# The last feed-forward of a two-layer decoder: the output product made transposed, in rounded halves, inside the sequence of wide products

## The chip, the cores and the metric

One core of one Trainium2 chip runs the whole program in one launch. Its engines work beside each other and meet only at semaphores: TensorE (PE in the rows; its weight loads stand apart as PEld), VectorE (DVE), ScalarE (ACT), GpSimd (POOL) and SyncE (SP), which starts the transfers. The metric is the device time of one execution in microseconds. It is compared as the median of several runs.

## What is computed

Two decoder layers in fp32 on `x` of 16 x 112 x 256. The change lies in the last step of the last layer, a feed-forward whose two largest of four gates choose a low-rank correction:

```python
logits = jnp.einsum('bsd,ed->bse', x, Wg) + bg
scores = jax.nn.softmax(logits, axis=-1)
topv, topi = jax.lax.top_k(scores, TOP_K)            # TOP_K = 2 of E = 4
w = jnp.sum(jax.nn.one_hot(topi, E) * topv[..., None], axis=-2)
base = jnp.einsum('bsd,fd->bsf', x, Wi)              # 256 -> 1024
lora = jnp.einsum('bser,efr->bsef', jnp.einsum('bsd,erd->bser', x, A), B)   # rank 4
h = jax.nn.relu(base[:, :, None, :] + lora)
expert_out = jnp.einsum('bsef,df->bsed', h, Wo)      # 1024 -> 256
out = jnp.einsum('bse,bsed->bsd', w, expert_out)
```

The `x` here is the normalised stream, and `out` is added to the stream itself. The output product is linear, so the kernel weighs the two chosen `h` of a token first and multiplies by `Wo` once.

## The kernel before

The function `l1_experts` is the last phase. It handles the 16 batch elements in four groups `g` of four, so a group has 4 x 112 = 448 tokens (`GT`). The 1024 inner features are cut into eight blocks `f` of 128 (`FC`), so the phase has 32 steps. Within one step of the loop over `f`:

- TensorE makes `z` (128 features x 448 tokens) in fp32 from two halves of the input (`multiply_wide`, L2774) and adds the first choice's low-rank term in one product of the rounded type fp32r (`multiply_low`, L2780). A second such product, `change` (L2786), holds the difference between the two choices.
- ScalarE copies `z` out of PSUM (`take_first`, L2724).
- VectorE adds `change` (L2663), applies relu and the weight ratio (L2666), and adds the first choice's relu (L2671). The result is block `f` of `h`. All eight blocks of a group are kept.

TensorE issues the wide and low product two blocks ahead. After the eight steps comes `project_out` (L2819): for each of the four batch elements eight fp32 products with the tokens' `h` as the weights and 256 columns of `Wo` moving, so that the output has tokens on the partitions. It is 32 products for a group, in one piece. VectorE weighs each result and adds the stream (`take_result`, L2679), and SyncE stores a group when its four results stand. Between the groups lie small things: `transpose_one_hot` (L2759) and `spread_ratio` (L2766) on TensorE, `mask_low` (L2623), `split_low` (L2629), `find_best` (L2642 to L2653) and `take_shares` (L2612 to L2615) on VectorE, `round_low` (L2713) and `take_ratio` (L2718) on ScalarE.

"Rounded halves" are a way to make an accurate product from the faster type: a number is written as a rounded part `hi` (a ScalarE copy into fp32r) and the rest `lo` (a subtraction), and three products hi x hi, lo x hi and hi x lo replace one fp32 product. The kernel does so already in the cross-attention of the first layer (L1037 to L1039, 488 columns, and L1046 to L1048, 512 columns).

Each engine runs its own list in the order written, and an instruction that waits holds up everything behind it on its engine. PSUM has eight banks of 512 columns: two for `z`, two for `change`, two for `y`, one each for the two one-hot tiles.

Of the kernel before, what the change touches and what calls it, by code (L numbers as in the profile page):

```python
# [7 lines left out]
F32 = mybir.dt.float32  # L8
# [2529 lines left out]
def l1_experts(nc, x, stats, norms, w, gate, ident, passed, A, out):  # L2538
# [16 lines left out]
    FIRST_SHARES, LAST_SHARES = slice(0, B - 2 * GB), slice(B - 2 * GB, B)  # L2555
# [4 lines left out]
    with ExitStack() as ctx:  # L2560
# [6 lines left out]
        h = ph.sb("h", [128, FC, GT])  # L2567
# [3 lines left out]
        z_ps, change_ps, y_ps = ph.banks("z", 2), ph.banks("change", 2), ph.banks("y", 2)  # L2571
# [12 lines left out]
        h_step, y_done, x_step = ph.sem("h_step"), ph.sem("y_done"), ph.sem("x_step")  # L2584

# [22 lines left out]
        @block.vector  # L2608
        def _(dve):
# [47 lines left out]
            def activate(g, f):  # L2657
                n = g * FC + f
# [4 lines left out]
                nc.vector.tensor_tensor(z_second[:, f % 2, :], z_first[:, f % 4, :], change_ps[:, f % 2, 0:GT], ALU.add  # L2663
                                        ).then_inc(h_step, 1)
# [4 lines left out]
                if f == 0:  # L2669
                    since(dve, y_done, g * GB)  # L2670
                nc.vector.scalar_tensor_tensor(h[:, f, :], z_first[:, f % 4, :], 0.0, z_second[:, f % 2, :], ALU.max, ALU.add  # L2671
                                               ).then_inc(h_step, 1)

            def take_result(g, j):
                b = g * GB + j
                dve.wait_ge(y_done, b + 1)
                if j == 0:
                    since(dve, stored[g % 2], g // 2 * 16)
                nc.vector.scalar_tensor_tensor(result[:, g % 2, j, :], y_ps[0:S, j % 2, 0:D], weight[:, b:b + 1], x[:, b, :],  # L2679
                                               ALU.mult, ALU.add).then_inc(x_step, 1)  # L2680
# [4 lines left out]
            take_shares(0, FIRST_SHARES)  # L2685
# [4 lines left out]
            for g in range(G):  # L2690
                for f in range(FC):
                    activate(g, f)
                    if g == 0 and f == 1:
                        take_gate()
                if g + 1 < G:
                    mask_low(g + 1)
                    split_low(g + 1)
                take_result(g, 0)
                if g == 0:
                    find_best(0, G - 2)  # L2700
                    find_best(1, G - 1)
                elif g == 1:
                    take_shares(1, LAST_SHARES)
                for j in range(1, GB):
                    take_result(g, j)

        @block.scalar
        def _(act):
# [17 lines left out]
            nc.scalar.activation(share[:, FIRST_SHARES], share[:, FIRST_SHARES], ACT.Exp).then_inc(exp_ready, 1)  # L2726
# [9 lines left out]
            for g in range(G):  # L2736
                for f in range(FC):
                    take_first(g, f)
                    if g == 0 and f == 2:
                        act.wait_ge(gate_done, 1)  # L2740
                        nc.scalar.activation(low[:, (G - 1) * GT:G * GT], y_ps[0:ER, 0, 0:GT], ACT.Copy).then_inc(low_ready, 1)
                if g + 1 < G:
                    round_low(g + 1)
                    if g == 1:
                        act.wait_ge(share_ready, 2)
                        nc.scalar.activation(share[:, LAST_SHARES], share[:, LAST_SHARES], ACT.Exp).then_inc(exp_ready, 1)
                    take_ratio(g + 1)

        @block.tensor
        def _(pe):  # L2750
# [11 lines left out]
            def spread_ratio(g):  # L2762
                pe.wait_ge(ratio_ready, 2 if g >= 2 else 1)
# [19 lines left out]
            def multiply_change(g, f):  # L2783
                n = g * FC + f
                since(pe, h_step, n * 3 - 5)
                nc.tensor.matmul(change_ps[:, f % 2, 0:GT], low_b_r[:, f * 128:(f + 1) * 128], low_change[:, g % 2],  # L2786
                                 start=True, stop=True).then_inc(change_done, 1)
# [9 lines left out]
            def multiply_gate():  # L2797
# [7 lines left out]
                for c in range(KC):  # L2805
                    done = nc.tensor.matmul(y_ps[0:ER, 0, 0:GT], low_a[:, c, :], x1T[:, c, (G - 1) * GT:G * GT],  # L2806
                                            start=(c == 0), stop=(c == KC - 1))
                done.then_inc(gate_done, 1)

            def project_out(g):  # L2810
                if g == 0:
                    pe.wait_ge(low_ready, 1)
                for j in range(GB):
                    b = g * GB + j
                    since(pe, x_step, b - 1)
                    for f in range(FC):
# [11 lines left out]
            for g in range(G):  # L2828
                multiply_low(g, 0)
                multiply_low(g, 1)  # L2830
                for f in range(FC):
                    multiply_change(g, f)
                    if f + 2 < FC:
                        multiply_wide(g, f + 2)
                        multiply_low(g, f + 2)
                    if g == 0 and f == 0:
                        multiply_gate()
                if g + 1 < G:
                    transpose_one_hot(g + 1)
                    multiply_wide(g + 1, 0)  # L2840
                    multiply_wide(g + 1, 1)
                project_out(g)
                if g + 1 < G:
                    spread_ratio(g + 1)

# [109 lines left out]
```

## Time and profile before

| | |
|---|---|
| Median of 3 runs | 1724.64 us (1720.76 to 1724.70) |
| Profiled execution, its own time | 1724.28 us |
| Its span in the trace | 1722.4 us |
| TensorE busy over the span | 1632.5 us (95%) |
| VectorE, ScalarE, GpSimd busy | 1084.2, 776.1, 544.8 us |
| Mean granted TensorE clock | 0.983 |
| Last feed-forward, first product to end of span | 1584.9 to 1722.4 us |

Rows of the timeline give the start of an instruction or of a run of equal ones, and its length. A TensorE record reaches from issue to the end of its pipeline, so records overlap: the price of a product in a dense stretch is the distance between starts, not the length. An fp32 product has two matmul records; an fp32r product has one. Span and own time differ by 1.88 us that lie outside the trace.

### The profile page before, as it was taken

How to read it: one execution, taken by the hardware profiler on the slowest of the kernel's cores; microseconds unless marked ns; L12 is line 12 of the kernel's file. 1: busy time of each engine (PE TensorE's matmuls, PEld its weight loads, DVE VectorE, ACT ScalarE, POOL GpSimd, SP SyncE). 2: the span in 40 equal slices, each digit the busy share in tenths (PEclk: the TensorE clock that was granted, in tenths of full speed). 3: DMA queues.
4: the chain of work that ended last, by engine and by line, in shares of the span. 5: the costliest groups of instructions: out<-in, count | busy, mean ns of one | idle time of the engine just before them, and what ended most of it. 6: DMA issues, size and time to landing. Idle time of an engine off the chain costs nothing. (4 is left out here: it accounts for less than half of the span.)

```text
span 1722.4 us, 33298 instructions
## 1 busy us (share of the span) xinstructions
PE 1632.5 (95%) x11494; PEld 1313.1 (76%) x11494; DVE 1084.2 (63%) x2543; ACT 776.1 (45%) x2178; POOL 544.8 (32%) x581
## 2 busy tenths in 40 slices
PE   6999899999999999999999988899988899988998
PEld 6877678778778878777887866799977777655666
DVE  5566467666777666667676664455354578856664
ACT  2356354444454455454545441365402577743211
POOL 1022223333333333333333334244430033354000
PEclk9999999999999999999999999899998999998999
DMA  3100300000000000000001004575310000010000
GB/s 102 48 11 1 117 12 11 11 10 10 0 10 10 10 10 10 8 2 10 10 10 55 11 2 167 140 255 191 104 64 21 25 2 2 2 60 1 11 11 22
DMA packets 48808, 67.46 MB, mean 39 GB/s; under 512 B 11826, under 2 KB 42770, under 8 KB 46034
## 3 DMA queue, kind: packets, MB, share of 16 engines
q1 hardware_dynamic: 47186, 62.66, 11.6%
q0 software_dynamic: 1536, 3.67, 0.7%
q8 instruction: 51, 0.84, 0.2%
q14 instruction: 35, 0.29, 0.1%
HBM read 57.02 MB, written 9.31 MB: 39 GB/s over the span
## 5 line engine op out<-in xcount | busy, mean ns | idle before, releaser
L709 POOL TENSOR_TENSOR l0x_p<-l0x_p,l0x_inv 112x488 f32<-112x488 f32 x256 | 261.7, 1043 | 426.4 <-DVE l0x_inv L806 425.2
L934 ACT ACTIVATE l0x_p<-l0x_s,l0x_low 112x488 f32<-112x488 f32 x256 | 177.9, 696 | 255.3 <-DVE l0x_low L795 222.6
L795 DVE CUSTOM_DVE_ANT_0 l0x_s<-l0x_score_ps,l0x_bias 112x488 f32<-112x488 f32 x256 | 160.2, 664 | 95.0 <-PE l0x_score_ps L1081 85.7
L1102 PE MATMUL l0x_oT_ps<-l0x_pT,l0x_v 122*64 122x112 f32 x2048 | 127.2, 266 | 7.0 <-ACT l0x_pT L940 6.1
L1089 PEld LDWEIGHTS l0x_pT_ps<-ident,l0x_p 112*122 112x122 f32 x1024 | 99.0, 138 | 45.3 <-issue 39.2
L1102 PEld LDWEIGHTS l0x_oT_ps<-l0x_pT,l0x_v 122*64 122x64 f32 x2048 | 99.6, 137 | 42.5 <-issue 31.8
L1089 PE MATMUL l0x_pT_ps<-ident,l0x_p 112*122 112x112 f32 x1024 | 126.1, 266 | 0.4 <-POOL l0x_p L709 0.3
L782 DVE TENSOR_TENSOR l0x_kT_lo<-l0x_proj_ps,l0x_kT_hi 128x488 fp32r<-128x488 f32 x128 | 84.1, 667 | 63.2 <-ACT l0x_kT_hi L924 63.2
L1037 PE MATMUL l0x_proj_ps<-l0x_kvT_hi,l0x_wkv_hi 128*128 128x488 f32 x256 | 104.7, 409 | 2.9 <-DVE l0x_kvT_lo L770 2.9
L1046 PE MATMUL l0x_proj_ps<-l0x_wkv_hi,l0x_kvT_hi 128*122 128x512 f32 x256 | 105.2, 411 | 0.0
L1047 PE MATMUL l0x_proj_ps<-l0x_wkv_lo,l0x_kvT_hi 128*122 128x512 f32 x256 | 101.0, 395 | 0.0
L1048 PE MATMUL l0x_proj_ps<-l0x_wkv_hi,l0x_kvT_lo 128*122 128x512 f32 x256 | 100.9, 394 | 0.0
L1039 PE MATMUL l0x_proj_ps<-l0x_kvT_hi,l0x_wkv_lo 128*128 128x488 f32 x256 | 99.4, 388 | 0.0
L1038 PE MATMUL l0x_proj_ps<-l0x_kvT_lo,l0x_wkv_hi 128*128 128x488 f32 x256 | 99.3, 388 | 0.0
L924 ACT ACTIVATE l0x_kT_hi<-l0x_proj_ps 128x488 fp32r<-128x488 f32 x128 | 72.9, 571 | 27.5 <-PE l0x_proj_ps L1039 27.4
L801 DVE COPY l0x_pT<-l0x_pT_ps 122x448 f32<-122x448 f32 x128 | 79.2, 619 | 4.6 <-PE l0x_pT_ps L1089 4.6
L1731 PE MATMUL l0f_hT_ps<-l0f_xsT,l0f_w 128*128 128x128 f32 x672 | 80.2, 279 | 0.0
L1731 PEld LDWEIGHTS l0f_hT_ps<-l0f_xsT,l0f_w 128*128 128x128 f32 x672 | 78.3, 195 | 0.0
L2040 POOL TENSOR_TENSOR l1a_pn<-l1a_p_even,l1a_inv 112x896 f32<-112x896 f32 x16 | 26.9, 1683 | 137.8 <-POOLq L1887 99.0
L211 ACT ACTIVATE l0a_p<-l0a_p,l0a_shift 112x112 f32<-112x112 f32 x128 | 47.8, 374 | 45.9 <-DVE l0a_shift L201 45.6
L940 ACT ACTIVATE l0x_pT<-l0x_pT_ps 122x448 f32<-122x448 f32 x128 | 66.7, 521 | 1.8 <-PE l0x_pT_ps L1089 1.8
L218 POOL TENSOR_TENSOR l0a_pn<-l0a_p,l0a_inv 112x896 f32<-112x896 f32 x16 | 26.9, 1683 | 120.3 <-DVE l0a_inv L206 120.3
(392 smaller groups left out, 4045.6 us busy)
## 6 DMA issues: line engine op xcount, KB each, us to landing
l0f_w<-in_l0f_w SPq DMA_DIRECT2D x21, 1024.0 KB
l0x_c_in<-in_ctx SPq DMA_DIRECT2D x16, 375.0 KB
l1x_gram_context<-in_ctx SPq DMA_DIRECT2D x16, 375.0 KB
sorted_x<-l0x_zeros SPq DMA_DIRECT2D x1, 2816.0 KB, 15.3
l0f_xs<-sorted_x SPq DMA_DIRECT2D x21, 128.0 KB, 2.2
sorted_y<-l0f_z SPq DMA_DIRECT2D x21, 128.0 KB, 1.8
l0x_wkv<-in_l0x_wkv SPq DMA_DIRECT2D x2, 1024.0 KB, 9.2
x<-in_x SPq DMA_DIRECT2D x4, 448.0 KB, 7.8
```

The source lines that it names most:

```text
L709: nc.gpsimd.tensor_tensor(p[:, i % 2, a, :], p[:, i % 2, a, :], inv[:, i % 2, a:a + 1].broadcast_to([S, KEYS]), ALU.mult).then_inc(pn_read ...
L795: nc.vector.tensor_tensor_reduce(s_sb[:, h % 2, :], score_ps[0:S, h % 2, 0:KEYS], bias[:], -SCALE, 3.4e38, ALU.add, ALU.min, low[:, h:h + ...
L934: nc.scalar.activation(p[:, h // 2 % 2, h % 2, :], s_sb[:, h % 2, :], ACT.Exp, scale=-1.0, bias=low[:, h:h + 1], accum_out=total[:, h:h + ...
L1037: nc.tensor.matmul(out, wkv_hi[:, c, at], kvT_hi[:, c, :], start=(c == 0), stop=False)
L1038: nc.tensor.matmul(out, wkv_hi[:, c, at], kvT_lo[:, c, :], start=False, stop=False)
L1039: done = nc.tensor.matmul(out, wkv_lo[:, c, at], kvT_hi[:, c, :], start=False, stop=(c == KC - 1))
L1046: nc.tensor.matmul(out, kvT_hi[:, c, keys], wkv_hi[:, c, at], start=(c == 0), stop=False)
L1047: nc.tensor.matmul(out, kvT_hi[:, c, keys], wkv_lo[:, c, at], start=False, stop=False)
L1048: done = nc.tensor.matmul(out, kvT_lo[:, c, keys], wkv_hi[:, c, at], start=False, stop=(c == KC - 1))
L1089: done = nc.tensor.transpose(pT_ps[0:KT, a, t * S:(t + 1) * S], p[:, i % 2, a, t * KT:(t + 1) * KT], ident[0:S, 0:S])
L1102: done = nc.tensor.matmul(oT_ps[a * DH:(a + 1) * DH, 0, (i % 4) * S:(i % 4 + 1) * S], v[:, t, (2 * i + a) * DH:(2 * i + a + 1) * DH], pT[: ...
L1731: done = nc.tensor.matmul(hT_ps[:, 2 * (i % 2) + f // 4, (f % 4) * 128:(f % 4 + 1) * 128], w1[:, i % 3, c, f * 128:(f + 1) * 128], xsT[:, ...
```

## The change

`project_out` is no longer a piece for a group. It becomes one of six products for each of the 32 steps, issued two steps after the step that made its `h`. `Wo` blocks are now the weights and `h` (448 columns) moves, so the output `yT` has features on the partitions. Operands are fp32r halves: `h_hi` comes from ScalarE (`round_h`), `h_lo` from VectorE (`split_h`). `Wo` is halved once at the start, by ScalarE and GpSimd. When a group's last block has been added, ScalarE copies `yT` out of PSUM (`take_yT`), TensorE turns it back (`transpose_back`: two transposes for a batch element, eight for a group, in two parts) and VectorE takes the results during steps 2 and 3 of the next group. `h` shrinks from eight blocks to two, `change` from two banks to one (its freed bank holds `back`). `find_best`, `take_shares`, `mask_low` and `split_low` are spread over steps 2 to 5. The shares are taken in three pieces instead of two.

```diff
+            for f in range(FC):
+                pool.wait_ge(wo_hi_ready, f + 1)
+                nc.gpsimd.tensor_tensor(wo_lo[:, f, :], wo[:, f, :], wo_hi[:, f, :].bitcast(F32), ALU.subtract
+                                        ).then_inc(wo_lo_ready, 1)
...
+            def split_h(n):
+                dve.wait_ge(h_hi_ready, n + 1)
+                nc.vector.tensor_tensor(h_lo[:, n % 3, :], h[:, n % 2, :], h_hi[:, n % 3, :].bitcast(F32), ALU.subtract
+                                        ).then_inc(h_lo_ready, 1)
...
-            for g in range(G):
-                for f in range(FC):
-                    activate(g, f)
-                    if g == 0 and f == 1:
-                        take_gate()
-                if g + 1 < G:
+            for n in range(STEPS):
+                g, f = divmod(n, FC)
+                activate(n)
+                if n >= 1:
+                    split_h(n - 1)
+                if n == 1:
+                    take_gate()
+                if g >= 1 and f in (2, 3):
+                    take_result(g - 1, 2 * f - 4)
+                    take_result(g - 1, 2 * f - 3)
+                if f == 2 and 1 <= g <= 2:
+                    take_shares(g, SHARES[g])
+                if f == 3 and g + 1 < G:
                     mask_low(g + 1)
+                if f == 4 and g + 1 < G:
                     split_low(g + 1)
-                take_result(g, 0)
...
+                if f == 5 and g < 2:
+                    find_best(g, G - 2 + g)
+            split_h(STEPS - 1)
+            for j in range(GB):
+                take_result(G - 1, j)
...
+            take_first(0, 0)
+            take_first(0, 1)
+            for f in range(FC):
+                nc.scalar.activation(wo_hi[:, f, :], wo[:, f, :], ACT.Copy).then_inc(wo_hi_ready, 1)
+            for n in range(STEPS):
+                g, f = divmod(n, FC)
+                if n + 2 < STEPS:
+                    take_first(*divmod(n + 2, FC))
...
+                if g >= 1 and f == 1:
+                    take_yT(g - 1)
+                round_h(n)
...
             def multiply_change(g, f):
                 n = g * FC + f
-                since(pe, h_step, n * 3 - 5)
...
+                since(pe, h_step, n * 3 - 2)
...
-            def project_out(g):
-                if g == 0:
+            def project_out(n):
+                g, f = divmod(n, FC)
+                if n == 0:
+                    pe.wait_ge(wo_lo_ready, FC)
+                pe.wait_ge(h_lo_ready, n + 1)
...
+                hi, lo = h_hi[:, n % 3, :], h_lo[:, n % 3, :]
+                for c in range(KC):
+                    if f == 0:
+                        since(pe, yT_ready, (g - 1) * KC + c + 1)
+                    at = slice(c * 128, (c + 1) * 128)
+                    nc.tensor.matmul(y_ps[:, c, 0:GT], wo_hi[:, f, at], hi, start=(f == 0), stop=False)
+                    nc.tensor.matmul(y_ps[:, c, 0:GT], wo_lo[:, f, at], hi, start=False, stop=False)
+                    done = nc.tensor.matmul(y_ps[:, c, 0:GT], wo_hi[:, f, at], lo, start=False, stop=(f == FC - 1))
...
+            def transpose_back(g, part):
...
+                pe.wait_ge(yT_ready, (g + 1) * KC)
+                since(pe, x_step, g * GB + 2 * part)
+                for j in (2 * part, 2 * part + 1):
+                    for c in range(KC):
+                        at = (j % 2) * D + c * 128
+                        done = nc.tensor.transpose(back_ps[0:S, 0, at:at + 128], yT[:, c, j * S:(j + 1) * S], ident[:])
                     done.then_inc(y_done, 1)
...
+            for n in range(STEPS):
+                g, f = divmod(n, FC)
+                multiply_change(g, f)
+                if n + 2 < STEPS:
+                    multiply_wide(*divmod(n + 2, FC))
+                    multiply_low(*divmod(n + 2, FC))
...
+                if g >= 1 and f in (2, 3):
+                    transpose_back(g - 1, f - 2)
+                if n >= 2:
+                    project_out(n - 2)
```

TensorE at the end of group 0 in the kernel before: `l1f_z_ps` is the wide and low product, `l1f_y_ps` the output product, the rows with `ident` the small transposes.

```order
 L2774 MATMUL l1f_z_ps<-l1f_x1T,l1f_wi 128x448 x2
 L2780 MATMUL l1f_z_ps<-l1f_low_first,l1f_low_b_r 128x448
 L2786 MATMUL l1f_change_ps<-l1f_low_change,l1f_low_b_r 128x448 x2
 L2759 MATMUL l1f_first_hot_ps<-ident,l1f_one_hot 80x112 x4
 L2759 MATMUL l1f_change_hot_ps<-ident,l1f_one_hot 80x112 x4
 L2774 MATMUL l1f_z_ps<-l1f_x1T,l1f_wi 128x448 x4
 L2819 MATMUL l1f_y_ps<-l1f_wo,l1f_h 112x256 x32
 L2766 MATMUL l1f_change_hot_ps<-ident,l1f_ratio 128x112 x4
 L2780 MATMUL l1f_z_ps<-l1f_low_first,l1f_low_b_r 128x448 x2
```

TensorE in the changed kernel, step 2 of group 1, where the turning back stands (`l1f_back_ps`):

```order
 L2835 MATMUL l1f_change_ps<-l1f_low_change,l1f_low_b_r 128x448
 L2823 MATMUL l1f_z_ps<-l1f_x1T,l1f_wi 128x448 x2
 L2829 MATMUL l1f_z_ps<-l1f_low_first,l1f_low_b_r 128x448
 L2887 MATMUL l1f_back_ps<-ident,l1f_yT 112x128 x4
 L2871 MATMUL l1f_y_ps<-l1f_h_hi,l1f_wo_hi 128x448
 L2872 MATMUL l1f_y_ps<-l1f_h_hi,l1f_wo_lo 128x448
 L2873 MATMUL l1f_y_ps<-l1f_h_lo,l1f_wo_hi 128x448
 L2871 MATMUL l1f_y_ps<-l1f_h_hi,l1f_wo_hi 128x448
 L2872 MATMUL l1f_y_ps<-l1f_h_hi,l1f_wo_lo 128x448
 L2873 MATMUL l1f_y_ps<-l1f_h_lo,l1f_wo_hi 128x448
```

The 32 products in one row have become six in each step, and the wide product no longer runs ahead of a long piece.

VectorE in the changed kernel, steps 2 and 3 of the last group (`l1f_h_lo` is `split_h`, `l1f_result` is `take_result`; the kernel before has the three lines of a step alone and `l1f_result` x4 after the last step):

```order
 L2678 SCALAR_TENSOR_TENSOR l1f_z_second<-l1f_z_second,l1f_ratio_rows 128x448
 L2681 SCALAR_TENSOR_TENSOR l1f_h<-l1f_z_first,l1f_z_second 128x448
 L2686 TENSOR_TENSOR l1f_h_lo<-l1f_h,l1f_h_hi 128x448
 L2694 SCALAR_TENSOR_TENSOR l1f_result<-l1f_back_ps,l1f_weight,x 112x256 x2
 L2675 TENSOR_TENSOR l1f_z_second<-l1f_z_first,l1f_change_ps 128x448
 L2678 SCALAR_TENSOR_TENSOR l1f_z_second<-l1f_z_second,l1f_ratio_rows 128x448
```

A step has four long operations on VectorE instead of three, and results stand between the steps.

ScalarE in the changed kernel, from the first step of group 2 (`l1f_h_hi` is `round_h`, `l1f_yT` is `take_yT`):

```order
 L2744 ACTIVATE l1f_z_first<-l1f_z_ps 128x448
 L2764 ACTIVATE l1f_yT<-l1f_y_ps 128x448 x2
 L2758 ACTIVATE l1f_h_hi<-l1f_h 128x448
 L2744 ACTIVATE l1f_z_first<-l1f_z_ps 128x448
 L2758 ACTIVATE l1f_h_hi<-l1f_h 128x448
```

The copy of `yT` stands ahead of step 1's rounding, which waits behind it.

## Rows read from the trace of the kernel before

**Rows 1.** The page: engines over the span; busy us, share, instructions.
```profile
PE 1632.5 (95%) x11494; PEld 1313.1 (76%) x11494; DVE 1084.2 (63%) x2543; ACT 776.1 (45%) x2178; POOL 544.8 (32%) x581
```
**Rows 2.** Windows of the last phase: length, busy PE, PEld, DVE, ACT, POOL, clock, DMA.
```profile
1584.00:1600.00 16.00, 14.30 (x66) 9.70 (x66) 5.97 (x17) 7.10 (x14) 1.82 (x3) 0.86 0.01 1
...
1612.20:1626.10 13.90, 13.90 (x66) 11.37 (x65) 7.41 (x38) 1.11 (x2) 1.72 (x2) 1.00 0.01 2
```
**Rows 3.** Timeline, group 0: start, length, engine, line, out<-in.
```profile
1595.65 0.54 ACT L2724 ACTIVATE l1f_z_first<-l1f_z_ps 128x448 f32<-128x448 f32 x1 [1.62 <-PE l1f_z_ps L2780]
1600.41 0.36 PE L2786 MATMUL l1f_change_ps<-l1f_low_change,l1f_low_b_r 80*128 80x448 f32 x1
...
1602.33 0.36 PE L2786 MATMUL l1f_change_ps<-l1f_low_change,l1f_low_b_r 80*128 80x448 f32 x1
...
1602.53 1.67 PE L2774 MATMUL l1f_z_ps<-l1f_x1T,l1f_wi 128*128 128x448 f32 x4
1602.79 0.62 DVE L2663 TENSOR_TENSOR l1f_z_second<-l1f_z_first,l1f_change_ps 128x448 f32<-128x448 f32 x1
1603.45 0.62 DVE L2666 SCALAR_TENSOR_TENSOR l1f_z_second<-l1f_z_second,l1f_ratio_rows 128x448 f32<-128x448 f32 x1
...
1608.05 0.57 PE L2786 MATMUL l1f_change_ps<-l1f_low_change,l1f_low_b_r 80*128 80x448 f32 x2
...
1608.46 0.55 PE L2759 MATMUL l1f_first_hot_ps<-ident,l1f_one_hot 112*80 112x112 f32 x4
```
**Rows 4.** Timeline, between groups 0 and 1, TensorE alone.
```profile
1609.23 3.19 PE L2774 MATMUL l1f_z_ps<-l1f_x1T,l1f_wi 128*128 128x448 f32 x8
1612.25 13.98 PE L2819 MATMUL l1f_y_ps<-l1f_wo,l1f_h 128*112 128x256 f32 x64
1626.07 1.04 PE L2766 MATMUL l1f_change_hot_ps<-ident,l1f_ratio 112*128 112x112 f32 x8
1626.88 0.65 PE L2780 MATMUL l1f_z_ps<-l1f_low_first,l1f_low_b_r 80*128 80x448 f32 x2
1627.37 0.37 PE L2786 MATMUL l1f_change_ps<-l1f_low_change,l1f_low_b_r 80*128 80x448 f32 x1
1628.18 1.77 PE L2774 MATMUL l1f_z_ps<-l1f_x1T,l1f_wi 128*128 128x448 f32 x4 [0.44 <-ACT l1f_z_first L2724]
```
**Rows 5.** Timeline, rounded products of the first layer's cross-attention, 488 columns.
```profile
602.01 0.38 PE L1038 MATMUL l0x_proj_ps<-l0x_kvT_lo,l0x_wkv_hi 128*128 128x488 f32 x1
...
604.22 0.39 PE L1039 MATMUL l0x_proj_ps<-l0x_kvT_hi,l0x_wkv_lo 128*128 128x488 f32 x1
```
**Rows 6.** Timeline, VectorE and ScalarE at the end of group 0.
```profile
1611.69 0.62 DVE L2671 SCALAR_TENSOR_TENSOR l1f_h<-l1f_z_first,l1f_z_second 128x448 f32<-128x448 f32 x1
1612.23 0.61 DVE L2623 TENSOR_TENSOR l1f_low_masked<-l1f_low,l1f_first_hot_ps 80x448 f32<-80x448 f32 x1
...
1612.88 0.58 ACT L2713 ACTIVATE l1f_low_first<-l1f_low_masked 80x448 fp32r<-80x448 f32 x1 [4.08 <-DVE l1f_low_masked L2623]
1613.41 0.58 ACT L2713 ACTIVATE l1f_low_change<-l1f_low_masked 80x448 fp32r<-80x448 f32 x1
1613.49 0.62 DVE L2629 TENSOR_TENSOR l1f_low_first<-l1f_low_masked,l1f_low_first 16x448 fp32r<-16x448 f32 x1
```
**Rows 7.** Timeline, GpSimd and VectorE in the phase before, two groups of it.
```profile
1546.76 3.20 POOL L2271 TENSOR_TENSOR l1x_y_in<-l0f_x,l1x_rows 112x256 f32<-112x256 f32 x4
...
1548.01 2.63 DVE L2354 SCALAR_TENSOR_TENSOR l1x_z<-l1x_y,l1x_y_mv,l1x_rows 112x256 f32<-112x256 f32 x4
...
1558.98 2.79 POOL L2271 TENSOR_TENSOR l1x_y_in<-l0f_x,l1x_rows 112x256 f32<-112x256 f32 x4
...
1563.65 1.67 DVE L2354 SCALAR_TENSOR_TENSOR l1x_z<-l1x_y,l1x_y_mv,l1x_rows 112x256 f32<-112x256 f32 x4
```
**Rows 8.** Timeline, the end of the span.
```profile
1707.17 11.04 PE L2819 MATMUL l1f_y_ps<-l1f_wo,l1f_h 128*112 128x256 f32 x50 [1.08 <-DVE l1f_h L2671]
...
1718.25 0.48 DVE L2679 SCALAR_TENSOR_TENSOR l1f_result<-l1f_y_ps,l1f_weight,x 112x256 f32<-112x256 f32 x1 [2.97 <-PE l1f_y_ps L2819]
```

More of the change, by code:

```diff
@@ L2566, in l1_experts @@
         z_first, z_second = ph.sb("z_first", [128, 4, GT]), ph.sb("z_second", [128, 2, GT])
-        h = ph.sb("h", [128, FC, GT])
+        h = ph.sb("h", [128, 2, GT])
+        h_hi, h_lo = ph.sb("h_hi", [128, 3, GT], F32R), ph.sb("h_lo", [128, 3, GT], F32R)
+        wo_hi, wo_lo = ph.sb("wo_hi", [128, FC, D], F32R), ph.sb("wo_lo", [128, FC, D], F32R)
+        yT = ph.sb("yT", [128, KC, GT])
         result = ph.sb("result", [S, 2, GB, D])
-        z_ps, change_ps, y_ps = ph.banks("z", 2), ph.banks("change", 2), ph.banks("y", 2)
+        z_ps, change_ps, y_ps = ph.banks("z", 2), ph.banks("change", 1), ph.banks("y", 2)
+        back_ps = ph.banks("back", 1)
         first_hot_ps, change_hot_ps = ph.banks("first_hot", 1), ph.banks("change_hot", 1)
@@ L2735, in _ @@
             nc.scalar.activation(x1T[:, :, (G - 1) * GT:G * GT], y_ps[:, :, 0:GT], ACT.Copy).then_inc(xT_ready, 1)
[L2736 to L2742, printed above, removed]
+            take_first(0, 0)
[7 more added lines that the diff above has]
+                if n == 0:
+                    act.wait_ge(gate_done, 1)
+                    nc.scalar.activation(low[:, (G - 1) * GT:G * GT], back_ps[0:ER, 0, 0:GT], ACT.Copy).then_inc(low_ready, 1)
+                if g >= 1 and f == 1:
+                    take_yT(g - 1)
+                round_h(n)
+                if f == 0 and 1 <= g <= 2:
+                    weigh_shares(g)
+                if f == 3 and g + 1 < G:
                     round_low(g + 1)
-                    if g == 1:
-                        act.wait_ge(share_ready, 2)
-                        nc.scalar.activation(share[:, LAST_SHARES], share[:, LAST_SHARES], ACT.Exp).then_inc(exp_ready, 1)
+                if f == 5 and g + 1 < G:
                     take_ratio(g + 1)
+            take_yT(G - 1)
         @block.tensor
@@ new lines, in transpose_back @@
+            def transpose_back(g, part):
+                if g == 0 and part == 0:
+                    pe.wait_ge(low_ready, 1)
+                pe.wait_ge(yT_ready, (g + 1) * KC)
+                since(pe, x_step, g * GB + 2 * part)
+                for j in (2 * part, 2 * part + 1):
+                    for c in range(KC):
+                        at = (j % 2) * D + c * 128
+                        done = nc.tensor.transpose(back_ps[0:S, 0, at:at + 128], yT[:, c, j * S:(j + 1) * S], ident[:])
@@ L2827, in _ @@
             transpose_last()
[L2828 to L2838, printed above, removed]
+            multiply_low(0, 0)
+            multiply_low(0, 1)
+            for n in range(STEPS):
+                g, f = divmod(n, FC)
+                multiply_change(g, f)
+                if n + 2 < STEPS:
+                    multiply_wide(*divmod(n + 2, FC))
+                    multiply_low(*divmod(n + 2, FC))
+                if n == 0:
+                    multiply_gate()
+                if g >= 1 and f in (2, 3):
+                    transpose_back(g - 1, f - 2)
+                if n >= 2:
+                    project_out(n - 2)
+                if f == 2 and g + 1 < G:
                     transpose_one_hot(g + 1)
[L2840 to L2843, printed above, removed]
+                if f == 5 and g + 1 < G:
                     spread_ratio(g + 1)
+            project_out(STEPS - 2)
+            project_out(STEPS - 1)
+            transpose_back(G - 1, 0)
+            transpose_back(G - 1, 1)
 def program(nc, A, out):
```

67 lines of the change are left out of this document (38 added, 29 removed).

## The prediction

> **What bounds the kernel now.** I read the page's first part: TensorE is busy 95% of the span [rows 1]. That alone says little, so I laid out the last phase in the timeline. Inside a group, `change` starts at 1600.41 and again at 1602.33 with TensorE never idle; over the steps that follow the distance is 1.905 us, since from the start at 1600.41 to the one at 1608.05 there are four steps, 7.64 us [rows 3]. So a step costs TensorE 1.905 us, VectorE and ScalarE wait for it. One rounded product of 448 columns costs 0.205 us: two stand between 1608.05 and 1608.46 [rows 3]. The wide product is the rest, 1.905 - 2 x 0.205 = 1.495 us for two fp32 products. After the eight steps, the 32 output products run from 1612.25 to 1626.07, 13.82 us, or 0.432 each, with no gap [rows 4]. Behind them TensorE is briefly starved: `change` starts at 1627.37 and the next wide product only at 1628.18, 0.6 us more than its own price [rows 4]. The clock is at 2.4 GHz in that stretch (granted 1.00); at the phase's beginning it is 0.86 of it on average [rows 2]. TensorE's work is therefore what sets the end, down to the last result at 1718.25 [rows 8].
>
> **Removed.** 128 fp32 products x 0.432 = 55.3 us of TensorE, all on the path. Three joints between groups of 0.6 to 0.7 us each, since the next group's wide product is now issued while the old group's output is still being made: 2 us. Before the last group's output TensorE waits for `h` as well: 1707.17 is such a start [rows 8]; about 1.5 us.
>
> **Added on TensorE.** 32 steps x 6 rounded products. Price from 0.205 us (same width, 80 rows) [rows 3]. The nearest rows with 128 rows and this very pattern of halves have 488 columns: ten intervals from 602.01 to 604.22, 0.221 us each [rows 5]. Scaled by the columns that is 0.203; unscaled 0.221 is the upper end. I take 0.205: 192 x 0.205 = 39.4 us, upper end 42.4, lower end 38. A step is then 1.905 + 1.23 = 3.135 us. The turning back is 32 transposes; eight similar ones (112 wide instead of 128) take 1608.46 to 1609.23, 0.77 us [rows 3, 4], so 0.77 for a group.
>
> **The start.** Up to step 1 nothing on TensorE changes, and both kernels should meet at the `change` of step 2, 1600.41 [rows 3]. What is new must be ready by its output products at 1600.41 + 1.905 = 1602.3. ScalarE now rounds eight blocks of `Wo` (256 columns) before its third `take_first`, which stood at 1595.65 [rows 3]. An activation from SBUF of 448 columns follows its like after 0.53 us [rows 6], so eight take 3 to 4 us from 1594.1 and end by 1598.4; the third `take_first` slips to 1598.9, and its reader, the wide product two steps on, comes at 1600.6. Hidden, with 1.7 us to spare. GpSimd subtracts eight blocks: a 112 x 256 one costs 2.79 / 4 = 0.70 us [rows 7], 5.6 us from 1594.5, end 1600.1. But in the phase before, where GpSimd and VectorE each read two SBUF tensors at once, four GpSimd operations took 3.20 instead of 2.79 us and four of VectorE 2.63 instead of 1.67 [rows 7]. VectorE runs five such operations here. So the end can move to 1601 to 1603.4, and `h_lo` of step 0, due at about 1601.5, can slip by 1 us. I take 0.5 us of waiting on TensorE, bounds 0 and 1.5.
>
> The Trainium skill ("SBUF — State Buffer", section "SBUF: two separate sides") says more: one of the two engines holds the shared port pair for its whole instruction and the other blocks. If the trace followed that fully, 5.6 us and five operations of 0.62 us would stand in line to 1603.2, and the wait would be 0.9 us instead of 0.5. Rows 7 show a part of this, the sign agrees.
>
> **The middle.** From 1600.41: steps 2 to 29 are 28 x 3.135 = 87.8 us. To it come, three times each, the one-hot transposes (0.77), the spreading of the ratio (1626.07 to 1626.88, 0.81 [rows 4]) and the turning back (0.77): 7.05 us. With the 0.5 us, step 30 starts at 1695.7.
>
> Does VectorE keep up? An operation that waits for the one before starts 0.66 us after it (1602.79 and 1603.45, [rows 3]), one that does not, 0.54 us after (1611.69 and 1612.23, [rows 6]). A step is then add, multiply, maximum and `split_h`: 0.66 + 0.66 + 0.54 + 0.54 = 2.40 us against 3.135. Rounding the rest of `h` is like L2629, 0.62 us long at the same width [rows 6]. The small operations of a group are at most the 7.41 us that stand beside the first output piece [rows 2]. So 8 x 2.40 + 7.4 = 26.6 against 8 x 3.135 + 2.35 = 27.4 us on TensorE: it keeps up, by little. The small ones land in steps 2 to 5, where VectorE has 4 x 0.735 = 2.9 us to spare and TensorE's own extras give 2.35: 2.1 us late at the worst. It may be some 2 us late: the single `change` bank lets TensorE go on when the add is done (0.46 + 0.62 us into a step of 3.135), and `h_lo` of step n is ready 3 us into step n + 1 and wanted 1.9 us into step n + 2, 2.0 us later. In groups 0 and 1 the two meet: 0 to 0.2 us each, which I leave out; if VectorE's operations were a tenth longer it would be about 1.5 us each, and that is the upper end, 3 us.
>
> A rule of the Trainium skill ("VectorE: DVE Perf Modes", section "The DRAIN you can't avoid") has a semaphore between two operations cost nothing. The rows say 0.12 us each. By the rule a VectorE step would be 2.16 us, and the tail below 0.6 us shorter.
>
> ScalarE has two 0.53 us operations a step. Its long wait is at step 1 of a group: `take_yT` waits for TensorE's end of the step, and `round_h` of step 1 waits behind it. It is done 1.7 us into step 2; VectorE wants it some 2.5 us into step 2. Hidden; its cover is gone if TensorE is ahead of VectorE by nothing. `transpose_back` in step 2 waits for both copies, ready 1.2 us in, and stands 1.7 us in behind the wide product: also hidden.
>
> **The tail.** After 1695.7 there is no wide product to hide behind. Counted from there, by the intervals above: the step's add 0.46, its `h` done 2.40, `h_lo` of step 29 done 2.93 (TensorE, at 1.64, waits 1.3), step 31's `h` done 4.79, `h_lo` of step 30 done 5.32 (TensorE waits 1.2 more), of step 31 6.06. The last six products run 6.58 to 7.98, the copies of `yT` end at 8.56, the first four transposes at 9.12, two results at 10.1, and only then may the second four go, since `back` has one bank: results end at 11.6. TensorE does 6.1 us of work in these 11.6. So the last result ends at 1707.3, where it was 1718.73 [rows 8]; from there to the end of the span lie 3.67 us of storing in both. Span 1711.0, own time 1711.0 + 1.88 = 1712.9 against 1724.28 of the profiled execution; the median lies 0.4 above that one, so **1713**. A second way to count it: 55.3 + 2 + 1.5 - 39.4 - 3.1 = 16.3 us, less 0.5 at the start and 5 of idle at the end, is 10.8 us, beside 11.4 the first way. This difference is my rounding.
>
> **Rivals.**
> - *VectorE becomes the bound.* For it: 26.6 against 27.4 us leaves 3%, and the clustering in steps 2 to 5. Against it: TensorE has room for a lag of 2 us. Each VectorE operation 10% longer costs 3 us (1716); 20% longer makes VectorE set the pace in three groups, 8 x 0.48 - 0.8 = 3 us for each, 9 in all with the tail's 1: 1723. I give 0.15 to 1716 to 1719.5 and 0.06 to more.
> - *Slower than before: the rounded products do not overlap with their weight loads.* Each of the 192 has its own load now, where a load served a longer product. If each took its record's whole length, 0.38 us [rows 5], that is 192 x 0.175 = 33.6 us more: 1746. It decides from 0.264 us a product on. Against it: rows 5 have records of 0.38 and starts every 0.22. 0.04.
> - *The sequence does not do what it says*: the shorter products come, but TensorE waits in each step for the chain over VectorE, ScalarE and VectorE to `h_lo`. The chain has a whole step of room by the count above; 0.3 us a step would be 10 us, 1722. 0.03.
> - *More than forecast*: products at 0.195, no wait at the start, less in the tail: 1710. Part of the forecast's own range.
>
> **How the numbers follow.** The forecast, 1710 to 1716, has 0.72. Before's three runs spread over 4 us, which also enters. The range 1709 to 1718.5 takes in the product price (-1.5, +3), the start (+1) and most of the VectorE case. About 0.3% is what a measurement of this kernel can tell from no change, 5.2 us: faster is below 1719.5. Faster 0.72 + 0.15 = 0.87; the third rival and half of the heavy VectorE case are within, 0.08; slower 0.05.
>
> **What would show it.** Right: `change` every 3.1 to 3.15 us in steady steps; six starts of L2871 to L2873 0.205 apart; VectorE busy 75% to 95% in the phase; TensorE idle over 1 us only after the last wide product; the first output product at about 1602.8. Wrong: idle time of TensorE before L2835 (the `change` bank) or L2871 (`h_lo`) in steps 4 to 7 of groups 0 and 1; product starts over 0.22 apart; a tail of more than 12 us from step 30 to the last result.

## The result, and the profile after

| | before | changed |
|---|---|---|
| Median of 8 runs | 1725.32 us (1720.76 to 1728.20) | 1714.65 us (1709.31 to 1722.63) |
| Profiled execution: own time, span | 1724.28, 1722.4 us | 1714.85, 1713.0 us |
| `change` of step 2 to end of the last result | 1600.41 to 1718.73: 118.32 us | 1600.19 to 1709.40: 109.21 us |

The ratio is 0.9948, with a 95% interval of 0.9932 to 0.9965, which lies below 1: faster, by half a per cent. The third line of the table is the measure of most that follows, because the eight runs of each kernel spread over 7 and 13 us and part of that arises before this phase: over the profiled executions, whose code before the phase is the same, its first product starts at 1582.11 to 1588.85. I call that third line **the stage**.

From the page of the changed kernel, its engines (busy us, share of the span, instructions), to be read beside [rows 1]:

```profile
PE 1622.8 (95%) x11462; PEld 1309.2 (76%) x11462; DVE 1100.7 (64%) x2578; ACT 800.7 (47%) x2227; POOL 552.0 (32%) x589
```

TensorE has 9.7 us less, VectorE 16.5 and ScalarE 24.6 us more, and TensorE still is the engine that sets the end. The window over the dense part of the phase (length, then busy time with instructions of PE, PEld, DVE, ACT and POOL, granted clock, DMA share, GB/s):

```profile
1602.30:1694.00 91.70, 91.70 (x396) 67.96 (x394) 81.06 (x170) 37.06 (x71) 1.76 (x2) 1.00 0.05 16
```

TensorE is busy for all of the 91.70 us and VectorE for 88% of them. The timeline of TensorE at the start of the phase and of a step later, the counterpart of [rows 3]:

```profile
1600.19 0.36 PE L2835 MATMUL l1f_change_ps<-l1f_low_change,l1f_low_b_r 80*128 80x448 f32 x1
...
1602.09 0.37 PE L2871 MATMUL l1f_y_ps<-l1f_h_hi,l1f_wo_hi 128*128 128x448 f32 x1
1602.30 0.37 PE L2872 MATMUL l1f_y_ps<-l1f_h_hi,l1f_wo_lo 128*128 128x448 f32 x1
...
1607.23 0.36 PE L2835 MATMUL l1f_change_ps<-l1f_low_change,l1f_low_b_r 80*128 80x448 f32 x1
...
1610.36 0.36 PE L2835 MATMUL l1f_change_ps<-l1f_low_change,l1f_low_b_r 80*128 80x448 f32 x1
...
1695.62 0.36 PE L2835 MATMUL l1f_change_ps<-l1f_low_change,l1f_low_b_r 80*128 80x448 f32 x1
```

The first output product stands 1.90 us after `change`, so it waits for nothing. The six products start 0.20 to 0.21 us apart, a step takes 3.13 us, and step 30 starts at 1695.62. GpSimd and VectorE at the start, while `Wo` is halved; the second line is the view of the tile `l1f_wo_lo` (shortest, median and longest of the eight, in ns):

```profile
1594.17 6.66 POOL L2612 TENSOR_TENSOR l1f_wo_lo<-l1f_wo,l1f_wo_hi 128x256 fp32r<-128x256 f32 x8 [7.69 <-ACT l1f_wo_hi L2779]
...
L2612 POOL TENSOR_TENSOR l1f_wo_lo<-l1f_wo,l1f_wo_hi x8: 724/733/1121, 1594.2 to 1599.7; 128x256 fp32r<-128x256 f32 x8
...
1594.70 1.04 DVE L2681 SCALAR_TENSOR_TENSOR l1f_h<-l1f_z_first,l1f_z_second 128x448 f32<-128x448 f32 x1
...
1600.28 1.04 DVE L2681 SCALAR_TENSOR_TENSOR l1f_h<-l1f_z_first,l1f_z_second 128x448 f32<-128x448 f32 x1
1601.24 0.61 DVE L2686 TENSOR_TENSOR l1f_h_lo<-l1f_h,l1f_h_hi 128x448 fp32r<-128x448 f32 x1
...
1603.16 0.63 DVE L2681 SCALAR_TENSOR_TENSOR l1f_h<-l1f_z_first,l1f_z_second 128x448 f32<-128x448 f32 x1
```

Eight subtractions take 6.66 us. Their mean of 0.83 hides two kinds: five are 0.72 to 0.73 us long and start 0.68 us apart, about as the undisturbed ones in [rows 7], and the three that stand beside VectorE's L2678 and L2681 (at 1594.17, 1595.22 and 1599.71) take 1.09 to 1.12. VectorE's L2681 takes 1.04 us there and 0.63 afterwards. GpSimd ends at 1600.83, 1.3 us before the first reader; `h_lo` of step 0 ends at 1601.85, only 0.24 us before its reader at 1602.09. Now the end of the phase, TensorE's waits first (us in brackets, behind them who released it):

```profile
1698.62 0.47 PE L2871 MATMUL l1f_y_ps<-l1f_h_hi,l1f_wo_hi 128*128 128x448 f32 x1 [1.20 <-DVE l1f_h_lo L2686]
...
1701.01 0.74 PE L2871 MATMUL l1f_y_ps<-l1f_h_hi,l1f_wo_hi 128*128 128x448 f32 x1 [0.88 <-DVE l1f_h_lo L2686]
...
1701.54 0.58 PE L2872 MATMUL l1f_y_ps<-l1f_h_hi,l1f_wo_lo 128*128 128x448 f32 x1
1701.92 0.58 PE L2873 MATMUL l1f_y_ps<-l1f_h_lo,l1f_wo_hi 128*128 128x448 f32 x1
...
1707.49 0.99 PE L2887 MATMUL l1f_back_ps<-ident,l1f_yT 128*112 128x128 f32 x4 [1.06 <-DVE l1f_result L2694]
1708.52 0.88 DVE L2694 SCALAR_TENSOR_TENSOR l1f_result<-l1f_back_ps,l1f_weight,x 112x256 f32<-112x256 f32 x2 [1.17 <-PE l1f_back_ps L2887]
```

And windows of the same kernel over that place (the last two lines are narrower ones):

```profile
1695.00:1701.00 6.00, 3.92 (x18) 2.93 (x16) 5.16 (x9) 1.74 (x4) 0.00 (x0) 0.98 0.00 0
1701.00:1705.00 4.00, 4.00 (x12) 3.42 (x12) 0.62 (x1) 0.44 (x2) 0.00 (x0) 0.60 0.00 0
1701.00:1704.00 3.00, 3.00 (x8) 2.72 (x9) 0.62 (x1) 0.02 (x1) 0.00 (x0) 0.50 0.00 0
1707.50:1708.50 1.00, 0.98 (x4) 0.57 (x4) 0.00 (x0) 0.00 (x0) 0.00 (x0) 0.55 0.00 0
```

The two waits were forecast, the rows behind the second are not: the products start 0.37 to 0.38 us apart instead of 0.205, and the granted clock is 0.50, the level of 1.2 GHz, from 1701 to 1704 (0.60 on average over four us). From 1704.4 on they stand 0.20 apart again. A second, smaller fall, to 0.55, lies over the last four transposes, behind their own wait of 1.06 us. The tail (step 30's `change` to the last result's end) is 13.78 us, where 11.6 was forecast.

### The profile page after: what moved, and what is told of

Its sections match the earlier page's. It is cut to its first block and busy times, and to the rows that moved or that the text cites. A ratio compares the mean times of both kernels' runs of the same rounds, so it can differ in the third digit from the quotient of the medians.

```text
span 1713.0 us, 33366 instructions
## 1 busy us (share of the span) xinstructions
PE 1622.8 (95%) x11462; PEld 1309.2 (76%) x11462; DVE 1100.7 (64%) x2578; ACT 800.7 (47%) x2227; POOL 552.0 (32%) x589
## 3 DMA queue, kind: packets, MB, share of 16 engines
q1 hardware_dynamic: 47186, 62.66, 11.8%
HBM read 57.02 MB, written 9.31 MB: 39 GB/s over the span
```

## The experiments

Each kernel was profiled once, the changed one twice. Its stage, its tail, and its ratio to the kernel before, whose tail includes the last piece of output products:

| kernel | stage, us | tail, us | ratio (95%) |
|---|---|---|---|
| before | 118.32 | 16.23 | 1 |
| changed, first profile | 109.21 | 13.78 | 0.9948 (0.9932 to 0.9965) |
| c0, changed again | 107.39 | 11.97 | 0.9942 (0.9918 to 0.9966) |
| e1, woven, fp32 | 113.81 | 10.81 | 0.9968 (0.9949 to 0.9986) |
| e6, one piece, transposed fp32 | 122.72 | 18.07 | 1.0025 (1.0014 to 1.0037) |
| e4, VectorE +1 operation a step | 113.16 | 13.10 | 0.9969 (0.9946 to 0.9992) |
| e3, tail filled | 107.34 | 11.96 | 0.9937 (0.9920 to 0.9954) |
| e8, longer waits | 111.63 | 16.26 | 0.9958 (0.9918 to 0.9998) |
| e9, longer waits, filled | 109.50 | 14.11 | 0.9964 (0.9943 to 0.9984) |
| e2, last three steps fp32 | 105.64 | 10.21 | 0.9917 (0.9896 to 0.9938) |
| e7, e2 and a shorter end | 104.71 | 9.31 | 0.9911 (0.9884 to 0.9938) |

### c0_changed: the same kernel once more

> The changed kernel itself, on the chip on which the next three run, so that they have a neighbour. Expected 9 to 12 us below the kernel before, span near 1713, the last feed-forward's tail (from the change product of step 30 to the last result) 13.4 us long.

Same ratio. The end of the phase in this second profile, timeline and a window:

```profile
1700.03 0.47 PE L2871 MATMUL l1f_y_ps<-l1f_h_hi,l1f_wo_hi 128*128 128x448 f32 x1 [0.90 <-DVE l1f_h_lo L2686]
...
1700.33 0.37 PE L2872 MATMUL l1f_y_ps<-l1f_h_hi,l1f_wo_lo 128*128 128x448 f32 x1
...
1705.73 0.88 DVE L2694 SCALAR_TENSOR_TENSOR l1f_result<-l1f_back_ps,l1f_weight,x 112x256 f32<-112x256 f32 x2 [0.81 <-PE l1f_back_ps L2887]
```

```profile
1700.00:1704.00 4.00, 3.34 (x16) 2.58 (x16) 0.63 (x1) 1.14 (x3) 0.00 (x0) 1.00 0.00 0
```

The same waits to 0.02 us, but the clock stays at 1.00 and the products at 0.20. The tail is 11.97 us, where I had expected 13.4. So the fall of the clock costs 1.8 us where it comes, and it does not come in every execution. Of the 1.8, about 1.45 lies between the first and the last of the twelve output products behind the second wait (3.78 us against 2.33) and 0.37 at the last four transposes (1.03 us from their start to the next result, against 0.66).

### e1_woven_fp32: the weaving without the rounding

```diff
-                    nc.tensor.matmul(y_ps[:, c, 0:GT], wo_hi[:, f, at], hi, start=(f == 0), stop=False)
-                    nc.tensor.matmul(y_ps[:, c, 0:GT], wo_lo[:, f, at], hi, start=False, stop=False)
-                    done = nc.tensor.matmul(y_ps[:, c, 0:GT], wo_hi[:, f, at], lo, start=False, stop=(f == FC - 1))
+                    done = nc.tensor.matmul(y_ps[:, c, 0:GT], wo[:, f, at], h[:, n % 3, :], start=(f == 0), stop=(f == FC - 1))
```

> The woven sequence and the transposed output are kept, the rounding is undone: the output product of a step is two fp32 products of 448 columns on h itself, nothing is rounded or split. Theory (the gain has three parts: orientation, rounding, weaving): an fp32 product of 448 columns costs 0.748 us, so a step of TensorE grows from 3.135 to 3.40 us, 28 steps by 7.4 us; the tail is shorter by about 3 us since no rounding stands in its chain and the clock does not fall. So about 4 us slower than the changed kernel and about 6 us faster than before. Rival (the rounded halves are the whole gain): as slow as before or slower. Rival (VectorE sets the pace of the changed kernel): faster than the changed kernel, since VectorE has three long operations instead of four.

The last step of the timeline (`change`, the four matmul records of the two output products, `change`):

```profile
1702.05 0.71 PE L2829 MATMUL l1f_change_ps<-l1f_low_change,l1f_low_b_r 80*128 80x448 f32 x1
...
1704.30 1.67 PE L2862 MATMUL l1f_y_ps<-l1f_h,l1f_wo 128*128 128x448 f32 x4
...
1705.46 0.71 PE L2829 MATMUL l1f_change_ps<-l1f_low_change,l1f_low_b_r 80*128 80x448 f32 x1
```

A step is 3.41 us, 0.27 more than with rounded halves; the tail is 1.2 us shorter, since no halves have to be made (and a little more than that, as a `change` behind an fp32 product is recorded early, 0.71 us long instead of 0.36). Against c0 the stage is 6.4 us longer.

### e6_piece_fp32: transposed output, still one piece for a group

```diff
-                if n >= 2:
-                    project_out(n - 2)
+                if g >= 1 and f == 1:
+                    for m in range((g - 1) * FC, g * FC):
+                        project_out(m)
```

Products in fp32 as in e1, ten blocks of `h` instead of three.

> As e1_woven_fp32 (transposed output in two fp32 products of 448 columns a step, nothing rounded), but the sixteen output products of a group are issued in one piece of 12.0 us, in step 1 of the next group, and not woven. VectorE's small operations stay in steps 2 to 5. Theory (weaving itself is worth what it hides of VectorE's and ScalarE's work): TensorE's products are the same, but a step now takes 1.905 us beside VectorE's 1.86 us, so the 2 to 6 us of small operations in steps 2 to 5 are no longer covered: TensorE waits about 2, 3 and 1 us in groups 0, 1 and 2, and the last group's twelve us of output follow its last h: about 6 us slower than e1_woven_fp32. Rival (TensorE's sum is all that counts, the order of it nothing): the same as e1_woven_fp32 within 1 us. Rival (weaving alone is the gain of the change, orientation nothing): as slow as the kernel before or slower.

TensorE's waits of this kernel (total, times, longest), and one of them in its timeline:

```profile
PE l1f_change_ps L2829 <- DVE l1f_z_second L2669: 5.7, 5, 1.6
```

```profile
1645.81 0.47 PE L2829 MATMUL l1f_change_ps<-l1f_low_change,l1f_low_b_r 80*128 80x448 f32 x1 [1.56 <-DVE l1f_z_second L2669]
```

By TensorE's price alone the transposed form is cheaper than before: 64 fp32 products of 448 columns, 0.748 each by the wide product's two in 1.495 us [rows 3], are 47.9 us where 55.3 were. Yet the stage is 4.4 us longer than before, and the ratio says slower as well, so 11.8 us have come on. With the output in one piece, TensorE's steps are 1.91 us again. VectorE's three operations of a step take about 1.86, and nothing is left for the small ones of steps 2 to 5; `find_best` alone stands 1.9 us long in step 5 (1610.10 to 1611.99). The single `change` bank passes that lag on to TensorE: 5.7 us. Turning back between the groups is 3 x 0.77 = 2.3 us by the forecast's price. The tail is 18.07 us where the kernel before has 16.23, although its products are 1.85 us cheaper: 3.7 us of turning back and copying behind the last piece.

From e6 to e1 the stage falls by 8.9 us and from e1 to c0 by 6.4; 4.4 - 8.9 - 6.4 = -10.9, the whole from before to c0. The 6.4 is the rounding, in a woven sequence. The 8.9 is not weaving alone: e6 keeps the small operations in steps 2 to 5, where the kernel before has them beside the long piece, so up to the 5.7 us of waits may belong to their place. A piece with the small operations beside it was not run, nor was rounding without weaving, which would need all eight blocks of `h_hi` and `h_lo` at once. I had expected 6 us between e6 and e1.

### e4_vector_once: one more VectorE operation a step

```diff
                     split_h(n - 1)
+                dve.wait_ge(h_step, n * 3 + 3)
+                for k in range(1):
+                    nc.vector.tensor_tensor(z_second[:, f % 2, :], h[:, n % 2, :], h[:, n % 2, :], ALU.add)
```

> The changed kernel with one more VectorE operation of 448 columns in each of the 32 steps, behind split_h, whose result nobody reads: 0.54 us more a step, 17.3 us in all. Theory (TensorE is the bound and VectorE has 3.135 - 2.40 = 0.73 us a step to spare, of which the small operations of steps 2 to 5 take nearly all): steps without small ones stay at 3.13 us; TensorE waits before change or before the output product in steps 4 to 7, nothing in group 0, about 2 us in group 1, 1 in group 2, 0 to 1 in group 3, and the tail grows by 1.1: 4 to 5 us slower than the changed kernel. Rival (VectorE already sets the pace): 15 to 17 us slower. Rival (VectorE has ample room): below 2 us.

Waits of TensorE in this kernel:

```profile
PE l1f_change_ps L2838 <- DVE l1f_z_second L2675: 2.8, 2, 1.4
PE l1f_y_ps L2874 <- DVE l1f_h_lo L2686: 3.0, 3, 1.4
```

In the tail of this kernel, timeline and a window:

```profile
1701.84 0.47 PE L2874 MATMUL l1f_y_ps<-l1f_h_hi,l1f_wo_hi 128*128 128x448 f32 x1 [1.24 <-DVE l1f_h_lo L2686]
...
1704.76 0.47 PE L2874 MATMUL l1f_y_ps<-l1f_h_hi,l1f_wo_hi 128*128 128x448 f32 x1 [1.43 <-DVE l1f_h_lo L2686]
...
1700.00:1708.00 8.00, 4.79 (x21) 3.44 (x20) 5.67 (x10) 2.20 (x4) 0.00 (x0) 1.00 0.00 0
```

The stage is 5.8 us longer than c0's: two steps of group 0 (4.72 and 3.42 us instead of 3.22 and 3.14) and two of group 1 (4.81 and 3.42 instead of 3.21 and 3.13) bring 3.7, the tail 1.1, the rest is spread; the forecast was 4 to 5. Thirty-two operations of more than 0.5 us are over 16 us, and about two thirds of it still fit beside TensorE. So TensorE is the bound, and VectorE's slack is real but small: 0.5 us a step is more than it holds in two of the four groups. I had expected no loss in group 0. The tail shows one thing more: waits of 1.24 and 1.43 us, longer than those of the changed kernel, and the clock stayed at 1.00.

### e3_tail_filled: the waits of the tail filled with unread products

```diff
+            def fill(count):
+                pe.wait_ge(first_ready, STEPS)
+                for k in range(count):
+                    nc.tensor.matmul(z_ps[:, 0, 0:GT], low_b_r[:, 0:128], low_change[:, (G - 1) % 2], start=True, stop=True)
```

Six stand ahead of step 29's output products and five ahead of step 30's.

> The changed kernel with eleven more rounded products in the tail whose results nobody reads (six before the output products of step 29, five before those of step 30), in the time in which TensorE waited. Theory (the waits bring the clock down): the clock stays at 1.00 in the last output products, which are 0.205 us apart instead of 0.373, and the span is about 1.5 us shorter than that of the changed kernel although TensorE does more. Rival (the clock falls there anyway, or the products are slow for another reason): the same span or up to 2 us more.

Tail 11.96 us, clock 1.00. That equals c0, which kept its clock without any filling, so the pair decides nothing. It led to the next two.

### e8_longer_waits and e9_longer_waits_filled

```diff
+                if n in (STEPS - 3, STEPS - 2):
+                    for c in range(KC):
+                        nc.vector.tensor_tensor(yT[:, c, :], ratio_rows[:, (G - 1) % 2], ratio_rows[:, (G - 1) % 2], ALU.add)
```

> The changed kernel with two more operations of 0.54 us on VectorE before split_h of step 29 and two before that of step 30, whose results nobody reads, so that TensorE waits longer in the tail: 2.3 us before the output products of step 29 (1.2 before) and 2.0 before those of step 30 (0.9). Theory (waits of TensorE bring its clock down, and the changed kernel stands at the edge: of two profiled executions one has the fall, one has not): the output products of steps 30 and 31 run 0.37 us apart, and the stretch from the change product of step 30 to the last result is 12.0 + 2.2 = 14.2 us plus 1.5 to 3. Rival (the fall in one execution was not due to the waits): 14.2 us and products 0.205 apart.

Timeline and windows of e8:

```profile
1697.46 0.47 PE L2874 MATMUL l1f_y_ps<-l1f_h_hi,l1f_wo_hi 128*128 128x448 f32 x1 [2.27 <-DVE l1f_h_lo L2689]
...
1700.91 0.74 PE L2874 MATMUL l1f_y_ps<-l1f_h_hi,l1f_wo_hi 128*128 128x448 f32 x1 [1.97 <-DVE l1f_h_lo L2689]
...
1701.45 0.57 PE L2875 MATMUL l1f_y_ps<-l1f_h_hi,l1f_wo_lo 128*128 128x448 f32 x1
1701.83 0.57 PE L2876 MATMUL l1f_y_ps<-l1f_h_lo,l1f_wo_hi 128*128 128x448 f32 x1
```

```profile
1693.00:1699.00 6.00, 3.67 (x17) 2.72 (x15) 5.21 (x10) 0.95 (x2) 0.00 (x0) 1.00 0.00 0
1699.00:1705.00 6.00, 4.09 (x11) 3.66 (x12) 2.39 (x5) 0.90 (x2) 0.00 (x0) 0.51 0.00 0
```

e9 is e8 with eleven and ten unread products in the two waits.

> As e8_longer_waits, and TensorE has eleven rounded products to do in the first of the two waits and ten in the second, whose results nobody reads. Theory (the waits bring the clock down): granted clock 1.00 and products 0.205 us apart up to the last output product, the stretch from the change product of step 30 to the last result 14.2 us. Rival: products 0.37 apart here too.

```profile
1703.62 2.19 PE L2896 MATMUL l1f_z_ps<-l1f_low_change,l1f_low_b_r 80*128 80x448 f32 x10
1705.74 0.47 PE L2874 MATMUL l1f_y_ps<-l1f_h_hi,l1f_wo_hi 128*128 128x448 f32 x1
1706.05 0.37 PE L2875 MATMUL l1f_y_ps<-l1f_h_hi,l1f_wo_lo 128*128 128x448 f32 x1
```

```profile
1698.00:1704.00 6.00, 5.93 (x29) 5.17 (x28) 5.21 (x11) 0.78 (x2) 0.00 (x0) 1.00 0.00 0
1704.00:1709.00 5.00, 4.44 (x21) 3.51 (x20) 2.22 (x5) 1.65 (x3) 0.00 (x0) 1.00 0.00 0
```

The pair speaks for idle time as the cause. After waits of 2.27 and 1.97 us with little work between them the granted clock is 0.51, the products stand 0.37 apart, and the tail is 16.26 us. With the same VectorE work and the waits filled, the clock stays at 1.00 and the tail is 14.11. But it is one execution of each, and c0 has shown that one kernel can come out either way. Over all profiles with waits left empty in front of the last output products (the changed kernel twice, e4, e8) the clock fell before the last of these products in two of four; with the waits filled or gone (e3, e9, e2, e7) it fell there in none. That idle time of TensorE takes the clock fits all of them and is not proven; why it comes in one execution of the changed kernel and not in the other, nor in e4, stays open. By the times e8 and e9 can't be told apart (1715.39 and 1717.74 us, overlapping intervals).

### e2_tail_fp32 and e7_short_end

e2 makes the last three steps' output in fp32, so that no halves are waited for:

```diff
+                    if whole:
+                        done = nc.tensor.matmul(y_ps[:, c, 0:GT], wo[:, f, at], h_block(n), start=False, stop=(f == FC - 1))
```

> The changed kernel, but the output products of the last three steps are fp32 products on h itself, without rounding and splitting. Theory (the missing 2 us of the forecast lie in the tail, where TensorE waits for h_lo twice and its clock then falls to the lower level): both waits before the output products of steps 29 and 30 go or shrink below 0.5 us, the granted clock stays at 1.00 until the last output product, whose start then lies about 3.4 us earlier; span 3 to 3.5 us shorter than the changed kernel. Rival (the clock falls for another reason, at that time of the kernel): the products are still 0.37 us apart and the gain is below 2 us.

```profile
1699.97 1.67 PE L2879 MATMUL l1f_y_ps<-l1f_yT,l1f_wo 128*128 128x448 f32 x4
...
1704.64 0.88 DVE L2697 SCALAR_TENSOR_TENSOR l1f_result<-l1f_back_ps,l1f_weight,x 112x256 f32<-112x256 f32 x2 [0.80 <-PE l1f_back_ps L2897]
```

TensorE no longer waits in front of an output product, and the clock is 1.00 up to the last one. The tail is 10.21 us, 1.8 less than c0's and 3.6 less than that of the changed kernel's first profile; the 3 to 3.5 us I expected were counted from the latter, with its fallen clock, and against c0, where no clock fell, the shorter chain is worth 1.8 (L2879 reads the last `h` from half of `yT`, which is free by then). e7 adds a second bank for the last four transposes and stores the last group in two halves:

```diff
+            for j in (0, 2):
+                b = (G - 1) * GB + j
+                sp.wait_ge(x_step, b + 2)
...
+                bank = change_ps if g == G - 1 and j >= 2 else back_ps
```

> The changed kernel with a shorter end: fp32 output products on h for the last three steps (as in e2_tail_fp32), the second four transposes of the last group into the freed bank of change instead of waiting for the results of the first four, and the last group stored in two transfers of two batch elements. Theory (all three waits of the tail are latency and can be taken out one by one): the tail from the change product of step 30 to the last result, 12.0 us in the changed kernel and 10.2 in e2_tail_fp32, becomes 9.4; the time from the last result to the end of the span, 3.6 us, gets 0.3 to 1 us shorter; median about 4 us below the changed kernel. Rival (the store is a fixed latency and the second bank does not help since VectorE is the bound there): the same as e2_tail_fp32.

```profile
1703.80 0.65 PE L2907 MATMUL l1f_back_ps<-ident,l1f_yT 128*112 128x128 f32 x4 [0.63 <-ACT l1f_yT L2771]
1704.28 0.60 PE L2907 MATMUL l1f_change_ps<-ident,l1f_yT 128*112 128x128 f32 x4
...
1705.28 0.87 DVE L2702 SCALAR_TENSOR_TENSOR l1f_result<-l1f_change_ps,l1f_weight,x 112x256 f32<-112x256 f32 x2
```

The second four transposes follow the first after 0.48 us, where they stood 1.7 us behind in c0. The tail is 9.31 us, and the store behind the last result 2.95 us instead of 3.6. Its median is 1710.43 us, ratio 0.9911: the lowest here, and below both kernels in the stage by 2.7 and 13.6 us. Its interval overlaps with c0's, so against the changed kernel the times alone don't prove it; the stage does, in one profile of each.

## Why the prediction was right, and where a step was off

- **The forecast as a whole** held: 1713 us against 1714.65 measured, span 1711.0 against 1713.0. The difference is in one term, the tail. One of the prediction's own signs of being wrong came true, a tail of more than 12 us (13.78); in c0 it is 11.97.
- **Price of a product.** 0.205 us forecast, 0.206 measured (1602.09 to 1603.12 for five intervals). Both neighbours led there, the product of the same width on 80 rows (0.205) and the wider one scaled by columns (0.203). The rival of weight loads that don't overlap is out.
- **Step.** 3.135 forecast, 3.13 measured; step 30 at 1695.7 forecast, 1695.62 measured. Part of that is luck: small errors cancel. The 0.5 us of waiting at the start did not come, the stage begins 0.2 us earlier than in the kernel before, and the extras between the steps took 95.43 - 87.8 = 7.6 us instead of 7.05. The small things cost a little more than their own length: the first full product behind a run of transposes stands 0.28 us ahead of the next one (1629.23 and 1629.51), not 0.205.
- **The start.** GpSimd took 6.66 us, more than the 5.6 of the count, but it began at 1594.17 and ended in time. ScalarE's eight copies took 2.56 us (1593.67 to 1596.23) where 3 to 4 were counted. The Trainium skill's rule ("SBUF — State Buffer", section "SBUF: two separate sides") has the sign right: both engines were slower side by side. The size it gives is not seen: if one had held the other off entirely, 5.6 us and five operations of 0.62 from 1594.5 would have ended at 1603.2; the trace has 1600.83. The wait that came nearest to being seen was not GpSimd's but that for `h_lo` of step 0, 0.24 us.
- **VectorE** kept up as counted: 88% busy, the add of step 6 in group 1 starts 2.0 us after its `change` (1643.99 and 1641.99), and the next `change` at 1645.20 still finds it done. e4 shows how near that was: 0.5 us more a step breaks it in groups 0 and 1. My count saw the danger in groups 0 and 1, which is where e4 broke; in the expectation of e4 I took group 0 out again, and was wrong there.
- **The tail, the mis-sized term.** 11.6 us forecast, 13.78 measured. The waits were right: TensorE starts again at 3.0 and 5.39 us after step 30's `change`, forecast 2.93 and 5.32. (The rows' 1.20 and 0.88 count from the end of the last record; counted by starts, as in the forecast, they are 1.36 and 1.05 beside 1.3 and 1.2.) Of the miss, 0.4 us is there in c0 too: the transposes start a little later and each hand-over costs some 0.1 us more. The other 1.8 us is the clock, which the forecast left out. I had priced TensorE's last products at the price of a dense stretch, though I had just forecast two waits in front of them. c0 gives its size; e8 and e9 speak for its cause and do not prove it.
- **The second count.** I had called the 0.6 us between the two ways of counting rounding. The stage fell by 9.11 us in the first profile and by 10.93 in c0, beside 11.4 and 10.8 forecast; which way was nearer, one profile without the fall doesn't decide.

## What to carry to other kernels

Where the step of one engine is hardly longer than that of the engine it feeds (1.905 and 1.86 us here), look at the order before making the long matrix work cheaper. Here the cheaper product form, in a piece and with the small operations left in the steps, lost 4 us (e6), and the same products woven into the steps won 9 over that. A form that needs a longer chain (rounded halves) pays in the middle and not at the end; the last steps, with nothing left to hide behind, are better in the short-chain form (e2, e7). Price products that stand behind waits like these, of about 1 to 2 us, with both levels of the clock.

## What was not expected of the hardware

- Waits of 1.20 and 0.88 us, with six products between them, were followed by a granted clock of 0.60 over the next 4 us in one execution and 1.00 in another of the same kernel. With 2.27 and 1.97 us it was 0.51. With 1.24 and 1.43 us (e4) it was 1.00: the length of the waits alone does not tell.
- VectorE's L2681 (448 columns, two tensors read from SBUF) went from 0.63 to 1.04 us beside GpSimd, and GpSimd's subtraction beside it from 0.73 to 1.12. The add L2675, which reads one of its two tensors from PSUM, kept its 0.62 (1598.75). Both slow down; neither stops for the other's whole instruction.
- The Trainium skill ("VectorE: DVE Perf Modes", section "The DRAIN you can't avoid") has a semaphore cost nothing between two VectorE operations. The measurement differs, and it decides: in c0's tail the multiply starts 0.65 us after the add it waits for (1695.11 and 1695.76), and an operation that needs nothing of the one ahead of it 0.53 to 0.55 us after it (1696.42 and 1696.97, 1696.97 and 1697.50), as in the rows of before.
